# Selection masks by VectorE and edge attributes turned one stage earlier, in a graph kernel with two message stages

## The reference

```python
# layer 0
relevant = segment_sum(x[dst_side_neighbour] * edge_weight, node, N)      # N x 128
x = layernorm(x + relevant @ W1 + (relevant * x) @ W2)
# layer 1, 8 heads of 16 features
e = edge_attr @ We + be                                                   # edge_attr: E x 64
logits = ((q[dst] * k[src]).sum(-1) + (q[dst] * e).sum(-1)) / 4
ex = exp(logits - segment_max(logits, dst)[dst])
attn = ex / segment_sum(ex, dst)[dst]
out = segment_sum(attn[..., None] * v[src], dst, N) @ Wo + bo
x = layernorm(x + out)
```

## Time and profile before

| what | us |
|---|---|
| median of the three runs | 13507.12 |
| the profiled execution | 13492.22 |
| its span | 13490.6 |

### The profile page before, as it was taken

How to read it: one execution, slowest core, us unless ns; L and a number is a source line. 1 busy time by engine, 2 the same in 40 slices (tenths; PEclk the granted TensorE clock), 3 DMA queues, 4 the chain that set the end, 5 groups by cost and what they waited for, 6 DMA issues and landing times. The chain is left out here.

```text
span 13490.6 us, 212064 instructions
## 1 busy us (share of the span) xinstructions
PE 7773.5 (58%) x49074; PEld 6032.7 (45%) x49074; DVE 5368.0 (40%) x19840; ACT 3708.5 (27%) x8489; POOL 8166.4 (61%) x6569
## 2 busy tenths in 40 slices
PE   2444444444444444445577777777777777777774
PEld 1433433343343333343355555555555555555552
DVE  3333333333333333334444444444444444444447
ACT  1111111111111111111144444444444444444441
POOL 2888888888888888884344444444444444444440
PEclk6666666666666666666777787777778777777786
DMA  8666666666666666665444444444444444444441
GB/s 195 105 105 107 106 106 105 107 105 105 106 106 106 105 107 106 105 107 141 129 121 122 123 122 122 122 121 122 121 121 124 120 122 121 121 123 122 120 122 44
DMA packets 2212139, 1558.78 MB, mean 116 GB/s; under 512 B 734904, under 2 KB 1995514, under 8 KB 2211832
## 3 DMA queue, kind: packets, MB, share of 16 engines
q0 software_dynamic: 628992, 668.10, 29.2%
q1 hardware_dynamic: 1519265, 835.24, 22.1%
q10 hardware_dynamic: 63832, 54.86, 1.4%
HBM read 1271.07 MB, written 286.16 MB: 115 GB/s over the span
## 5 line engine op out<-in xcount | busy, mean ns | idle before, releaser
L506 POOL DMA_INDIRECT rel_sum<-sums,row x3224 | 5003.5, 1552 | 1209.8 <-issue 624.0
L1087 POOL DMA_INDIRECT kv<-kv_rows,src_idx x3232 | 3084.2, 954 | 3493.3 <-DVE msg L1317 2566.9
L462 PE MATMUL coef_ps<-same,spread 128*128 128x128 f32 x6448 | 1634.6, 437 | 3572.7 <-DVE spread L435 2952.0
L462 PEld LDWEIGHTS coef_ps<-same,spread 128*128 128x128 f32 x6448 | 1423.2, 325 | 3749.9 <-DVE spread L435 3116.8
L1335 DVE TENSOR_TENSOR acc<-acc,out_ps 128x256 f32 x3232 | 1363.1, 422 | 1978.6 <-remote 889.5
L449 DVE TENSOR_TENSOR row<-moved,src_col 128x8 int32<-128x8 f32 x403 | 69.2, 172 | 3782.9 <-DMA rel_sum<-sums,row 3782.8
L1130 PE MATMUL ring_ps<-pick,q_win 128*128 128x128 f32 x6464 | 1259.5, 356 | 245.8 <-ACT pick L1420 186.9
L1130 PEld LDWEIGHTS ring_ps<-pick,q_win 128*128 128x128 f32 x6464 | 1101.9, 257 | 653.1 <-issue 648.9
L490 ACT ACTIVATE sums<-sum_ps 128x512 f32<-128x512 f32 x806 | 437.6, 595 | 2884.4 <-DMA rel_sum<-sums,row 2882.1
L435 DVE TENSOR_SCALAR spread<-iota_n,rel_col,w_col 128x128 f32<-128x128 f32 x3224 | 1213.1, 381 | 0.0
L431 DVE SCALAR_TENSOR_TENSOR same<-src_bc,src_col,later 128x128 f32<-128x128 f32 x3224 | 1114.2, 346 | 180.7 <-issue 118.5
(11 more groups left out here) (177 smaller groups left out, 7339.7 us busy)
## 6 DMA issues: line engine op xcount, KB each, us to landing
q_win<-q_rows SPq DMA_DIRECT2D x3232, 64.0 KB
src_bc<-src_flat SPq DMA_DIRECT2D x403, 512.0 KB
x_win<-in_x SPq DMA_DIRECT2D x3224, 64.0 KB
attr<-in_edge_attr SPq DMA_DIRECT2D x804, 128.0 KB
mark<-marks ACTq DMA_DIRECT2D x202, 256.0 KB
kv<-kv_rows,src_idx POOLq DMA_INDIRECT x3232
rel_sum<-sums,row POOLq DMA_INDIRECT x3224
rep<-rel_sum SPq DMA_DIRECT2D x100, 256.0 KB, 3.8
```

Source lines behind the costliest of these rows:

```text
L462: last = nc.tensor.matmul(coef_ps[k][:, i, :], spread[:, b, j, :], same[:, b, j, :], start=True, stop=True)
L506: pool.indirect_dma_start(out=rel_sum[r], out_offset=bass.IndirectOffsetOnAxis(ap=row[:, b, j:j + 1], axis=0), in_=sums[:, b, j, :], in_of ...
L1087: pool.indirect_dma_start(out=kv[:, 2 * i + u, k * S + s, :], out_offset=None, in_=kv_rows, in_offset=bass.IndirectOffsetOnAxis(ap=src_idx ...
```

## The change

In attention, the masks are written by VectorE. SyncE broadcasts the positions of a group's 2048 edges to all 128 partitions (bf16), and one instruction per quarter (`picks`) compares them with the number of the partition, `part`. The attributes are turned in the neighbours stage: there each group loads 1024 edges' attributes, TensorE transposes them, ScalarE copies them, and SyncE stores them to a table `attr_cols` (64 x edges) in device memory; attention loads `attr_t` from it directly, in two buffers. `num_rows`, two of the three `rel_rows`, `pick_fill`, `pick_drain`, `attr_fill` and `attr_drain` go. The ring's order is q2, q3, q0, q1.

```diff
 # prepare: 8 small VectorE instructions for num_rows and 6 on 128x3328 for rel_rows go
-                for m in range(3):
-                    sp.dma_start(rel_rows[m].rearrange("(c p e) -> p c e", p=P, e=P), rel_t[:, m]
-                                 ).then_inc(prep_stored, 16)
+                sp.dma_start(rel_flat.rearrange("(c p e) -> p c e", p=P, e=P), rel_t[:]).then_inc(prep_stored, 16)
 # neighbours, SyncE, between src_bc and x_win of group s
+                    wait_alone(sp, attr_filled, 2 * (s.g - 1), passed)
+                        sp.dma_start(attr[:, b, :, :], edge_attr[bass.ds(s.g * GP, GP), :].rearrange(
+                            "(p j) f -> p j f", j=G)).then_inc(attr_in[b], 16)
 # neighbours, SyncE, after x_win: keep_attr of group s - 1
+                    wait_alone(sp, attr_turned, 2 * s.g + 2, passed)
+                    sp.dma_start(attr_cols[:, bass.ds(s.g * GP, GP)], turned[:, b, :]).then_inc(attr_kept[b], 16)
 # neighbours, TensorE, between coef and sum matmuls
+                    wait_alone(pe, attr_in[b], ...)
+                    for k in range(2):
+                        wait_alone(pe, attr_turned, s.g * 2 - 1 + k, passed)
+                        for j in range(4):
+                            last = nc.tensor.transpose(attr_ps[k][:, j, :], attr[:, b, k * 4 + j, :], ident[:])
+                        last.then_inc(attr_filled, 1)
 # neighbours, ScalarE, between the copies to coef and to sums
+                        act.wait_ge(attr_kept[b], s.plus(-2).uses(2) * 16)
+                    for k in range(2):
+                        act.wait_ge(attr_filled, s.g * 2 + k + 1)
+                        nc.scalar.activation(turned[:, b, :].rearrange("f (p k j) -> f k j p", k=2, j=4)[:, k],
+                                             attr_ps[k][:], ACT.Copy).then_inc(attr_turned, 1)
 # attention
-PERIOD = (("q", 1, 2), ("q", 1, 3), ("pick", 2, 0), ("pick", 2, 1), ("attr", 2, 0), ("q", 2, 0), ("pick", 2, 2),
-          ("q", 2, 1), ("attr", 2, 1), ("pick", 2, 3))
+PERIOD = (("q", 1, 2), ("q", 1, 3), ("q", 2, 0), ("q", 2, 1))
 # set-up, VectorE
-                nc.vector.memset(rel[:], 0.0).then_inc(c_b, 1)
-                nc.vector.tensor_scalar(rel[:], rel[:], scrap[:, 0:1], None, ALU.add).then_inc(c_b, 1)
 # SyncE
-                    wait_alone(sp, attr_filled[u], n.plus(-1).count(), passed)
-                            sp.dma_start(attr[:, u, :, h, :], rows[2 * u + h]).then_inc(attr_in[u], 16)
+                    wait_alone(sp, ke_done[2 * u + 1], n.plus(-1).count(), passed)
+                            sp.dma_start(attr_t[h * ED:(h + 1) * ED, u, :, :], tiles[2 * u + h]).then_inc(attr_in[u], 16)
-                    wait_alone(sp, q_filled[3], n.plus(-3).count(), passed)
-                    sp.dma_start(rel[0:3, i, :], rel_rows[:, bass.ds(n.g * AP, AP)]).then_inc(rel_in[i], 16)
+                    wait_alone(sp, pick_ready[1], n.plus(-3).count(2), passed)
+                    for h in range(2):
+                        sp.dma_start(rel[h * ED:(h + 1) * ED, i, :], rel_flat[bass.ds(n.g * AP, AP)].rearrange(
+                            "(a e) -> a e", a=1).to_broadcast([ED, AP])).then_inc(rel_in[i], 16)
 # VectorE
+                def picks(n, k):
+                    i = n.slot
+                    if k == 0:
+                        dve.wait_ge(rel_in[i], n.landed(32))
+                    tiles = rel[:, i, :].rearrange("p (s q e) -> p q s e", q=B, e=P)[:, k]
+                    nc.vector.tensor_scalar(pick[:, k % 2], tiles, part[:, 0:1], None, ALU.is_equal
+                                            ).then_inc(pick_ready[k % 2], 1)
                         products(n, 2)
+                        picks(m, 0)
                         messages(c, 2)
                         products(n, 3)
+                        picks(m, 1)
                         add_bank(c, 1)
 ...
                         products(m, 0)
+                        picks(m, 2)
                         row_inflow(n)
                         row_peaks(n)
                         products(m, 1)
+                        picks(m, 3)
                         add_bank(c, 3)
 # TensorE: the calls of pick_fill and attr_fill go; keys waits for attr_in, q_fill for pick_ready
 # ScalarE: the calls of pick_drain and attr_drain go
```

More of the change, by code:

```diff
@@ L393, in neighbours @@
         sum_ps = [ctx.enter_context(nc.psum_tensor(f"sum_ps{i}", [P, 4, P], F32)) for i in range(2)]
+        attr_ps = [ctx.enter_context(nc.psum_tensor(f"attr_ps{i}", [ED, 4, P], F32)) for i in range(2)]
+        attr_in, attr_kept = ([sem(f"{n}{i}") for i in range(2)] for n in ("attr_in", "attr_kept"))
+        attr_filled, attr_turned = sem("attr_filled"), sem("attr_turned")
+        LEFT = (E - (NG - 1) * GP) // G
+        SPARE = E - (NG - 1) * GP - LEFT * G
+        assert 0 < LEFT and 0 < SPARE < G
         starts_in, src_in, x_in = sem("starts_in"), [sem(f"src_in{i}") for i in range(2)], [sem(f"x_in{i}") for i in range(2)]
@@ L1073, in _ @@
                 load_cols(Group(0, 1))
-                groups(sp, NG, HEAD, TAIL, {1: range(-2, 3)}, ((16 * U, 0), (16 * U, 1), (32, 1)), body)
+                groups(sp, NG, HEAD, TAIL, {1: range(-2, 3), 2: (-4, -2, 0)}, ((16 * U, 0), (16 * U, 1), (32, 1)), body)
             @block.gpsimd
@@ L1097, in bank_free, with attr_landed @@
                     (last_kind, at), then = two_back(kind, n, k)
-                    if last_kind == "pick" and then.is_from(0):
-                        pe.wait_ge(pick_drained[at % 2], then.count(2, 1 - at // 2))
-                    elif then.is_from(0):
-                        pe.wait_ge({"q": q_drained, "attr": attr_drained}[last_kind][at], then.count())
+                    if then.is_from(0):
+                        pe.wait_ge(q_drained[at], then.count())
                     return ring_ps[place_of(kind, k)[0] % 2]
-                def attr_fill(n, u):
+                def attr_landed(n, u):
                     full = n.is_under(NG - 1)
@@ L1110, in attr_fill @@
                         pe.wait_ge(attr_in[u], n.count(32, 32 - 16 * loads))
-                    to = bank_free("attr", n, u)
-                    for s in range(S):
-                        mm = nc.tensor.transpose(to[:, s, :], attr[:, u, s, :, :].rearrange("p h f -> p (h f)"), ident[:])
-                    mm.then_inc(attr_filled[u], 1)
-                def pick_fill(n, k):
-                    i = n.slot
-                    pe.wait_ge(rel_in[i], n.landed(16))
-                    to = bank_free("pick", n, k)
-                    rows = rel[:, i, :].rearrange("r (s q e) -> r q s e", q=B, e=P)[:, k]
-                    nc.tensor.matmul(to[:], num_rows[:], rows, start=True, stop=True).then_inc(
-                        pick_filled[k % 2], 1)
                 def q_fill(n, k):
@@ L1201, in body @@
                         q_fill(n, 3)
-                    if new:
-                        pick_fill(m, 0)
                     if old:
                         out_bank(c, 1)
-                    if new:
-                        pick_fill(m, 1)
-                        attr_fill(m, 0)
                     if mid:
@@ L1215, in body @@
                         out_bank(c, 2)
-                    if new:
-                        pick_fill(m, 2)
                     if mid:
@@ L1226, in body @@
                         out_bank(c, 3)
-                    if new:
-                        attr_fill(m, 1)
                     if mid:
@@ L1355, in body @@
                         products(n, 2)
+                    if new:
+                        picks(m, 0)
                     if old:
```

144 lines of the change are left out of this document (56 added, 88 removed).

## The result

| | before | after |
|---|---|---|
| median, four runs each | 13505.46 us | 13695.74 us |
| profiled execution: span | 13490.6 us | 13699.3 us |
| mean granted clock | 0.727 | 0.722 |

The ratio is 1.014, with a 95% interval of 1.0126 to 1.0154: 190 us slower, outside the range of the forecast (13,200 to 13,650), and not faster, as its likeliest case had it.

The account below looks back on a forecast made before the run. GpSimd was taken as the bound: its adds in neighbours, its gather batches, holding back completions, in attention. Terms -18 - 4 + 5 - 65 + 20 + 20 = -42 us gave 13,450, put at 13,460 (chance 0.50); range 13,200 to 13,650.

Parts of the forecast that it names:

- Prepare: Prepare stage: two of three stores go from the path, -18 us (0 to -19).
- Set-up of attention: Before attention: an instruction of 8.12 us and a memset go, -4 us (-2 to -11).
- Neighbours: Neighbours: new transposes and copies fit in idle time, added DMA may not be hidden, +5 us (0 to +190).
- third rival: Neighbours: the attributes' traffic delays the adds, +190 us instead of +5, so 13,645; chance 0.09.
- Attention, what goes: Attention: 3.25 us of TensorE and six ScalarE drains a group go, helping late intervals, -65 us (0 to -133).
- SyncE and the queues: Attention: attr_t loads that wait for `keys` and the positions' 512 KB cost 0 us (0 to +40).
- fourth rival: Attention: late intervals have another cause than TensorE's load, so -65 becomes 0 and 13,525 comes out; chance 0.13.
- Attention, what comes: Attention: VectorE's picks, 475 ns each, cost 0.1 us a group, +20 us (0 to +260).
- picks against gathers: Attention: more VectorE work slows gathers by 0.1 us a group, +20 us.
- Batches pace the stage: Attention: batches of 8 gathers (9.70 us) hold back other engines' completions and set the group's 32.57 us.
- TensorE's queue as the bound: Attention: all 3.25 us a group count, 656 us, so 12,870, or 13,200 with half; chance 0.14.
- Picks that hold gathers: Attention: picks stop GpSimd's gathers, +288 us instead of +20, so 13,728, or 13,580 with +139; chance 0.14.

Follow-up runs that it names:

- e6: Kernel after, neighbours' store on ScalarE's queue, copies plain, attention's picks, positions and attr_t loads cut: -44 us against the kernel before; neighbours 5987.8 us, attention -44.
- e5: Kernel after, neighbours' store in 8 pieces, attention's positions and picks cut, 16 transposes a group put back: +52 us against the kernel before; neighbours 5996.1, attention +42.
- e1: Kernel after, neighbours' attribute load and store and attention's positions cut to small pieces: -8 us against the kernel before; neighbours 5985.2 us, attention -1.
- e3: Kernel after, neighbours' attribute load and attention's positions and picks cut, store whole: +59 us against the kernel before; neighbours 6039.7 us, attention +12.
- e2: Kernel after, neighbours' store cut to 512 B and attention's picks to one column: +60 us against the kernel before; neighbours 5985.9 us, attention +69.
- e7: Kernel before with half the gathers, all other work the same: -1720 us against the kernel before, ratio 0.8709 to 0.8738.
- sets 3 to 5: Later groups of runs, on chips 14 and 7, where the kernel before takes 11,045 to 11,050 us.
- e10: Kernel before with each of attention's attribute loads cut from 128 rows to one: 0 us against the kernel before, on chips 14 and 7.
- g1: Whole change with only neighbours' store moved to ScalarE's queue: +56 us against the kernel before, on chips 14 and 7; neighbours 5989.0 us.
- h10: Repeat of e10, the kernel before with attention's attribute loads cut to one row each: +1 us against the kernel before.
- e9: Whole change with neighbours' store and attention's attr_t and positions loads on ScalarE's queue: +668 us against the kernel before; neighbours 5988.7 us.
- e4: Kernel after, most of neighbours' transposes and copies cut, 16 transposes a group added ahead of attention's q_fill: +462 us against the kernel before; attention +351.

## Why the prediction was wrong

The sum was -42 us; it came out as +190. By its own steps:

- **Prepare**, -18: -8.4 between the two traces. The stores went as said, but the one that stayed takes 11.20 us for 9.30, and the src_cols store came 10.0 us earlier, not 18. After the last store is issued, 14.9 us now pass until VectorE goes on, for 5.3 before: SyncE waits there for the landings, so they set the end and not the issuing, as the prediction had named as its doubt. Over all traces the first add comes at 228.6 us in the mean without the change's prepare and at 224.5 us with it, so the worth is nearer 4 us.
- **Set-up of attention**, -4: what lies between the last add and the first gather became 1.0 us shorter.
- **Neighbours**, +5: +148.5. This is the first step that failed, and the largest, with 143 of the 232 us between the sum and the result. "What is not hidden for sure is the DMA" was seen, and then the value was taken from the near end. That the bound of +190 held was luck: it priced every add at 1.61 us, but the adds kept 1551 ns, and the time came as waits for landings on 243 of 3223 adds. The third rival had the mechanism (late landings), borrowed its price from that bound, and with 13,645 came near. The reason given against it was wrong: I argued that src_bc's 512 KB are there already. The total of the bytes was not the point: 138 GB/s with the store on SyncE in rows of 4 KB cost 148 us, 141 GB/s with it on ScalarE's queue 1 us (e6), and in rows of 512 B on SyncE 10 us (e5). TensorE's 8 transposes were free, as predicted; ScalarE's copies took 1.12 us each and not 0.55, for they write with a stride, and were free as well (e1).
- **Attention, what goes**, -65, and **SyncE and the queues** for attr_t, 0: +12 together (e3). This is the second step that failed. Taken apart as -44 and +56 (e6) they would make the first right in kind, but e6 has no attribute loads where the kernel before has them. If the old loads cost as much as the new, the removed work is worth nothing, which is the fourth rival (the change gives attention nothing); if they cost nothing, it is worth 44 us. No run on the slower kind decides this.
- **Attention, what comes** and **picks against gathers**, +20 each: -13 to -19 for all of the picks (e1 against e3, the change against e2), within the error of nothing. A pick takes 493 ns, for 475.
- **SyncE and the queues** for the positions, 0 (0 to +40): +51 to +57 (e1 against the change, e3 against e2). This is the third step that failed: the transfer was called free because its due time is far. The parts -44, +56, +54 and -16 add up to the +50 of the whole, but they were found as differences along one row of runs, so they must; it is no check. What each transfer holds up in attention was not found.
- **Batches pace the stage**: right on the chips that stand at 13.5 ms (e7), and not a property of the kernel: on the chips of sets 3 to 5 it is not there. The reading behind it, that a result comes through with the batch's end, was made from one place. Of the 187 waits of VectorE for the spread of the carry (over 0.5 us, from 7000 us on, kernel before) 151 ended before the batch's last gather had started, and their median is 3.4 us. Results come late, and only sometimes with the end.
- Rivals: TensorE's queue as the bound did not come true, since removing 3.25 us a group gave 0.2 us at most (e6). Picks that hold gathers did not either.

The Trainium skill, page "SBUF — State Buffer", section "SBUF: two separate sides", let me give 0.14 to the picks. The trace shows such an effect in kind, as in the gather of 1.32 us, but of 725 gathers beside a pick only 125 took over 1.05 us. The mean rose by 7 ns, and without the picks attention was no shorter.

For the store the Trainium skill's page "DMA: Bandwidth & Descriptors", section "Queues, rings and completion order", has two rules: a DMA's semaphore increment lands only after every earlier write of the same DMA engine, across its queues, and a DMA engine takes turns between queues packet by packet. By the first, the adds' landings would wait for the store from whichever queue it comes. No run here tests it, because the one that changes the queue changes the moment as well: SyncE issues 256 KB of store, 512 KB of `src_bc` and 256 KB of attributes within some 2 us, and GpSimd's waits above 0.7 us end 8.1 us (median) after that store is issued, while ScalarE's store goes out some 10 us ahead of the next `src_bc`. Crowding alone is not enough either. The median peak over 4 us in each 15 us is 262 GB/s in the kernel after and 199 in e6, but also 255 in e2, which has the two loads without the store and lost nothing, and 258 in e5, which lost 10 us. Whether queue, moment or row length decides was not settled; a store on SyncE's queue at ScalarE's moment would tell.

Also open: whether attention's old attribute loads cost as much as the new ones on the slower kind of chip, and what makes the kinds differ.

## What to carry to other kernels

Where one engine's indirect DMAs pace a stage and each waits for the landing of an earlier one, a transfer added to it can't be priced by its bytes or its due time alone: try it from the other queue, at another moment and in shorter rows, before the design is judged. Do not take the value of an unknown cost from the near end of its bounds without a reason. Removing an eighth of the work of an engine that is busy 74% is worth little when its waits end with something else, and a pacing read off one chip should be checked on a second. When a run removes a part, make sure that it does not also remove something that the kernel before has.

## What the runs showed of the hardware

- On chips 0 and 5, while indirect gathers are issued, VectorE sees results of TensorE late: by 2.1 to 2.7 us in the medians of e1, e2, e5 and e6, and by 3.4 us in that of the kernel before (187 waits, up to 6.9 us). On chips 14 and 7 no such wait is there (e10, g1, h10), and attention takes 4140 us instead of 6561, at a granted clock of 1.00 instead of 0.79. Neighbours takes 5985 to 5987 us on both kinds.
- One and the same store of 256 KB in rows of 4 KB cost a stage paced by indirect adds 53 us (without the load, e3) or 148 us (with it) when SyncE issued it some 0.9 us ahead of a broadcast of 512 KB, and 1 to 2 us when ScalarE issued it some 10 us ahead of that (e6, e9, g1).
- A mean granted clock of 0.79 or 0.80 instead of 0.74 in attention, brought about by 16 more transposes a group, did not shorten the stage (e4, e5).
- A copy of 64x512 from PSUM takes 1.12 us when it writes one element every 32 bytes, and 0.59 us when it writes in a row (e6).
